# Mixture of experts in a two-layer kernel: 23 chunks of tokens sorted by expert instead of all tokens through all eight experts

## The chip, the cores and the metric

The kernel runs as one launch on one core of a Trainium2 chip. The metric is the device time of one execution in microseconds (us), as the median of repeated runs. Five engines work side by side, each with a queue of its own: TensorE (PE; its weight loads are PEld), VectorE (DVE), ScalarE (ACT), GpSimd (POOL) and SyncE (SP). SyncE, ScalarE and GpSimd also issue DMAs, which 16 DMA engines carry out.

## The reference

`x` has 2 batches of 2048 tokens of 256 features. Layer 0 is causal attention with 16 heads and a mixture of 8 experts, layer 1 a Toeplitz mixing of tokens and a gated feed-forward. Each of the four parts works on a normalised, modulated copy of `x` and is added back through a gate. Changed is the mixture:

```python
logits = einsum('bsd,de->bse', x, gate_w) + gate_b
probs = softmax(logits, axis=1)            # over the tokens of a batch
vals, idx = top_k(probs, 2)                # two experts for each token
h = relu(einsum('bsd,edo->ebso', x, w1) + b1[:, None, None, :])
h = relu(einsum('ebso,eop->ebsp', h, w2) + b2[:, None, None, :])
y = relu(einsum('ebso,eop->ebsp', h, w3) + b3[:, None, None, :])
onehot = one_hot(idx, E)
w_tok = einsum('bske,bsk->bse', onehot, vals)
ind = onehot.max(axis=2)
v = einsum('ebso,bse->eo', y, w_tok)       # one vector of 256 for each expert
out = einsum('bse,eo->bso', ind, v)
```

Three layers of 256x256 run over the tokens of each expert. What leaves an expert is one vector, the weighted sum over all its tokens of both batches; a token gets the sum of its two experts' vectors. A token that an expert was not chosen for has weight zero there.

## The kernel before

The phases follow one another: `phase_setup`, `phase_project`, `phase_attention`, `phase_attn_out`, `phase_route`, `phase_experts`, `phase_mix`, `phase_mix_out`, `phase_ffn`. Each is a block in which every engine has its own list of instructions, ordered by semaphores, and ends with all engines together. `x` stays in SBUF. A tile is 128 tokens, a chunk (CH) 512; the 4096 tokens are 8 chunks.

`phase_attention` is a hand-placed pipeline of 8 units (4 head groups by 2 batches). SyncE loads the heads, TensorE makes scores and running maxima, VectorE reduces maxima out of PSUM, ScalarE takes exponentials and copies finished outputs to `at_oc` (two buffers, L803), and GpSimd stores these to `d_o` (L623). Apart from one memset GpSimd does nothing else there. A unit has four outputs, in the order of 16, 12, 8 and 4 steps of the scores.

`phase_route` goes over the 8 chunks. For each, VectorE normalises (`ln_rows`, with a square root on ScalarE between its parts), TensorE transposes (L1116), ScalarE modulates to `ro_hf` (L1089), TensorE multiplies with the gate (L1126), ScalarE moves the logits to `ro_lg` (L1097), and GpSimd splits `ro_hf` into a high and a low f16 half, `hh_all` and `hl_all` (L1041, L1044), which stay in SBUF. VectorE has only the normalising in this loop. After it come the maxima over each batch, exponentials, scaling, transposes of the probabilities (L1135), the rank of each expert by all pairs of experts (L1072 to L1078), transposes of the indicator into `chosen`, and the weights `ro_wt`, which go to DRAM (L1028).

`phase_experts` goes over experts two at a time, and over 8 chunks of all 4096 tokens for each: 64 chunks of three layers. f32 is imitated by three f16 products (high by high, low by high, high by low), so a layer of a chunk is 12 matmuls of 128x512 and a chunk 36. `SEQ` sets the order on TensorE: in step s the first layer of chunk s, the second of chunk s-1, the third of chunk s-2. ScalarE adds bias and takes the relu into `ex_hf` (L1284), VectorE splits it (L1309, L1311); after the third layer VectorE multiplies by the token weights `ex_wb` (L1320, two instructions a chunk), which counts `dve_y`, and ScalarE takes the relu and sums (L1294). SyncE loads an expert's weights, biases and weights of all tokens once per expert, and GpSimd splits the weights (L1219, L1222). At the end two transposes and 32 tiles of small matmuls put the sums back on `x`.

## Time and profile before

| | |
|---|---|
| three runs | 2364.79, 2368.13 and 2371.26 us, median 2368.13 |
| profiled execution | 2367.53 us, of which the span is 2365.8 us |
| mean granted TensorE clock | 0.924 |
| busy in the span | PE 1989.2 (84%), PEld 957.3, DVE 1444.7 (61%), ACT 960.8 (41%), POOL 171.1 (7%) |
| DMA | 133.46 MB, mean 56 GB/s |

The span is the part of the execution that the profile records. Busy time is the time in which an engine runs at least one instruction. The granted clock is a share of full speed, 2.4 GHz; 0.5 is 1.2 GHz. Each group of instructions is named by line, engine, operation and output<-inputs. "Idle before" is the idle time of that engine just ahead of the group, and what ended it.

### The profile page before, as it was taken

How to read it: one execution, taken by the hardware profiler on the slowest of the kernel's cores; microseconds unless marked ns; L12 is line 12 of the kernel's file. 1: busy time of each engine (PE TensorE's matmuls, PEld its weight loads, DVE VectorE, ACT ScalarE, POOL GpSimd, SP SyncE). 2: the span in 40 equal slices, each digit the busy share in tenths (PEclk: the TensorE clock that was granted, in tenths of full speed). 3: DMA queues.
4: the chain of work that ended last, by engine and by line, in shares of the span. 5: the costliest groups of instructions: out<-in, count | busy, mean ns of one | idle time of the engine just before them, and what ended most of it. 6: DMA issues, size and time to landing. Idle time of an engine off the chain costs nothing. (4 is left out here: it accounts for less than half of the span.)

```text
span 2365.8 us, 37426 instructions
## 1 busy us (share of the span) xinstructions
PE 1989.2 (84%) x13666; PEld 957.3 (40%) x13666; DVE 1444.7 (61%) x3303; ACT 960.8 (41%) x1432; POOL 171.1 (7%) x133
## 2 busy tenths in 40 slices
PE   3773488999989999999956539999999998799978
PEld 3331022333333332333324214444444455699656
DVE  4664788787868787878302446767666655300366
ACT  0331045666666665666740224444444432100133
POOL 1001000000000000000003421111111000000011
PEclk8897599999999999999987669999999988899989
DMA  5236400303030303030013020111111000475001
GB/s 179 74 142 141 80 1 10 55 11 55 11 56 10 59 11 55 11 55 11 10 34 132 0 88 13 50 49 49 49 49 49 0 0 5 148 233 191 1 30 51
DMA packets 69129, 133.46 MB, mean 56 GB/s; under 512 B 9017, under 2 KB 52058, under 8 KB 62682
## 3 DMA queue, kind: packets, MB, share of 16 engines
q1 hardware_dynamic: 65344, 120.85, 18.5%
q0 software_dynamic: 2560, 8.39, 1.0%
q10 hardware_dynamic: 1090, 2.36, 0.3%
q8 instruction: 92, 1.51, 0.3%
q14 instruction: 43, 0.35, 0.1%
HBM read 99.83 MB, written 30.56 MB: 55 GB/s over the span
## 5 line engine op out<-in xcount | busy, mean ns | idle before, releaser
L812 ACT ACTIVATE at_pr<-ps 128x1024 f32<-128x1024 f32 (+3 forms) x640 | 548.8, 894 | 359.7 <-PE ps L752 230.5
L846 DVE TENSOR_REDUCE at_mx<-ps 128x1 f32<-128x512 f32 x768 | 488.8, 685 | 168.1 <-PE ps L702 158.4
L749 PE MATMUL ps<-at_sq,at_sk 64*128 64x512 f16 (+3 forms) x2560 | 344.5, 348 | 20.6 <-DMA at_sq<-at_mr 16.8
L702 PE MATMUL ps<-at_sk,at_sq 64*128 64x512 f16 (+3 forms) x1280 | 236.1, 365 | 112.3 <-DMA at_vl<-d_va 41.0
L728 PE MATMUL ps<-at_pr,at_vl 128*32 128x512 f32 (+3 forms) x2560 | 301.8, 543 | 0.5 <-issue 0.4
L1284 ACT ACTIVATE ex_hf<-ps,ex_bias 128x512 f32<-128x512 f32 x256 | 162.1, 684 | 282.0 <-PE ps L1253 243.8
L843 DVE CUSTOM_DVE_ANT_0 at_seen<-ps,later 128x384 bf16<-128x384 f32 (+3 forms) x512 | 229.9, 487 | 7.0 <-issue 5.3
L702 PEld LDWEIGHTS ps<-at_sk,at_sq 64*128 64x128 f16 x1280 | 62.0, 93 | 409.6 <-DVE at_mx L846 219.1
L752 PE MATMUL ps<-bq,bk 64*128 64x512 f16 (+3 forms) x1280 | 224.5, 347 | 0.0
L1253 PE MATMUL ps<-ex_hh,ex_wh 128*128 128x512 f16 x512 | 194.7, 380 | 12.5 <-DVE ex_hl L1311 11.6
L1309 DVE CAST ex_hh<-ex_hf 128x1024 f16<-128x1024 f32 x128 | 96.0, 750 | 165.7 <-ACT ex_hf L1284 165.7
L1253 PE MATMUL ps<-ex_hh,ex_wl 128*128 128x512 f16 x512 | 194.6, 380 | 0.0
L1253 PE MATMUL ps<-ex_hl,ex_wh 128*128 128x512 f16 x512 | 194.6, 380 | 0.0
L1311 DVE TENSOR_TENSOR ex_hl<-ex_hf,ex_hh 128x1024 f16<-128x1024 f32 x128 | 170.6, 1333 | 4.4
L749 PEld LDWEIGHTS ps<-at_sq,at_sk 64*128 64x128 f16 x2560 | 112.2, 95 | 126.3 <-ACT at_pr L812 35.7
L1516 PE MATMUL ps<-mi_vn,mi_tz 128*128 x1024 | 144.0, 303 | 1.3 <-DMA mi_tz<-d_z 1.3
L1516 PEld LDWEIGHTS ps<-mi_vn,mi_tz 128*128 128x128 f32 x1024 | 141.4, 191 | 4.1 <-issue 1.7
L1253 PE MATMUL ps<-hh_all,ex_wh 128*128 128x512 f16 x256 | 97.7, 382 | 20.5 <-POOL ex_wl L1222 15.7
L1253 PE MATMUL ps<-hh_all,ex_wl 128*128 128x512 f16 x256 | 97.8, 382 | 0.0
L1253 PE MATMUL ps<-hl_all,ex_wh 128*128 128x512 f16 x256 | 97.7, 382 | 0.0
L1441 DVE COPY mixed<-ps 128x256 f32 x32 | 13.6, 424 | 131.5 <-PE ps L1516 131.5
L1320 DVE SCALAR_TENSOR_TENSOR ex_h<-ps,ex_bias,ex_wb 128x512 f32<-128x512 f32 x128 | 89.8, 743 | 6.2 <-PE ps L1253 6.2
(199 smaller groups left out, 2114.8 us busy)
## 6 DMA issues: line engine op xcount, KB each, us to landing
mi_tz<-d_z SPq DMA_DIRECT2D x32, 1024.0 KB, 5.1
ex_wb<-d_wt SPq DMA_DIRECT2D x8, 2048.0 KB, 9.5
d_va<-pj_va SPq DMA_DIRECT2D x8, 1024.0 KB, 3.9
at_vl<-d_va SPq DMA_DIRECT2D x8, 1024.0 KB, 12.6
d_o<-at_oc POOLq DMA_DIRECT2D x32, 256.0 KB, 2.3
ex_w<-in_w SPq DMA_DIRECT2D x24, 256.0 KB, 3.1
x<-in_x SPq DMA_DIRECT2D x2, 2048.0 KB
at_sq<-d_qh SPq DMA_DIRECT2D x32, 128.0 KB, 8.3
```

The source lines that it names most:

```text
L702: ins = pe.matmul(ps[:, MAXB + (slot + r) % RING, 0:hi_ - lo], sq[half[r], b, i, 0, qb * P:(qb + 1) * P], sk[half[r], b, i, 0, lo:hi_], st ...
L728: ins = pe.matmul(ps[32 * h:32 * h + 32, O, off:CH], vl[:, b, kb, 32 * h:32 * h + 32], pr[:, n % 2, h // 2, h % 2, off:CH], start=(kb == 0 ...
L749: pe.matmul(ps[:, 2 * f + r, off:CH], sk[half[r], b, f, part, k], sq[half[r], b, f, part, q], start=part == 0, stop=False)
L752: ins = pe.matmul(ps[:, 2 * f + r, off:CH], g.bk[half[r], b, k], g.bq[half[r], b, q], start=False, stop=t < 0)
L812: act.activation(pr[:, n % 2, f, :, off:CH], ps[:, 2 * f:2 * f + 2, off:CH], ACT.Exp, scale=INV_SCALE).then_inc(exp_done[f], 1)
L843: ins = dve.tensor_tensor_reduce(seen[:, turn, r, 0:n], src, g.later[:, CH - n:CH], 1.0, LOWEST, ALU.add, ALU.max, dst)
L846: ins = dve.tensor_reduce(dst, src, AX.X, ALU.max)
L1253: ins = pe.matmul(ps[:, 2 * PAIR[l, cc] + o, :], lhs, rhs, start=(i == 0), stop=(i == len(parts) - 1))
L1284: ins = act.activation(hf[l][:, o, :], ps[:, 2 * PAIR[l, cc] + o, :], ACT.Relu, bias=bias[:, cc // NC_, l, o:o + 1])
L1309: dve.tensor_copy(hh[l][:, cc % 2], hf[l][:, :, :]).then_inc(high[l], 1)
L1311: dve.tensor_tensor(hl[l][:, cc % 2], hf[l][:, :, :], hh[l][:, cc % 2], ALU.subtract)\
L1516: ins = pe.matmul(ps[:, 2 * p + b, d * HD:C], tz[:, p, b, d * P:(d + 1) * P], vn[:, b * NT:(b + 1) * NT - d, bass.ds((it * 2 + p) * HD, HD ...
```

## The change

- **Weights**: in `phase_attention` GpSimd loads each of the 24 expert matrices, splits it into f16 halves and stores them in `d_w`; it also writes zeros over all of `d_rows`, one piece after each store of `at_oc`.
- **Routing**: TensorE transposes the modulated chunk back to token rows; ScalarE copies the high half and VectorE takes the low half, into a row of 264 words per token (`rows`: 512 f16 values, a weight, padding). The rank of all pairs becomes two rounds of a maximum with ties broken by a falling weight. Two matmuls count the tokens ahead of each; a scan over tiles and one over experts make a position for each token and choice, with each expert's range starting on a multiple of 512.
- **Scatter**: GpSimd scatters the 32 tiles of `rows` by the first choice, then by the second, each an indirect DMA of 128 rows to `d_rows`. VectorE puts in the second weight when the first scatter of eight tiles has landed.
- **Experts**: 23 chunks (NCK = 8192/512 + 7) of `d_rows`, each with its owner's weights; four buffers. Every chunk loads its weights (786 KB), its rows transposed (524 KB), and its 512 weights, first packed together in DRAM, then broadcast. All 23 chunks are always worked through. The tail sums the vectors of each expert's chunks with a small matmul.

```diff
+NCK = NB * T * 2 // CH + E - 1
+ROW = C + 8
@@ phase_attention, gpsimd
+            pool.wait_ge(ld[0], 16 * NLD)
+            fetch(0)
+            for n in range(3 * E):
+                e, l = divmod(n, 3)
+                x = n % 2
+                if n + 1 < 3 * E:
+                    fetch(n + 1)
+                pool.wait_ge(pw_ld[x], 16 * (n // 2 + 1))
+                if n >= 2:
+                    pool.wait_ge(pw_st[x], 16 * (n // 2))
+                pool.tensor_tensor(ph[:, x, 0], pw[:, x], one[:, :, :].to_broadcast([P, KT, C]), ALU.mult)\
+                    .then_inc(pw_high, 1)
+                pool.wait_ge(pw_high, n + 1)
+                pool.tensor_tensor(ph[:, x, 1], pw[:, x], ph[:, x, 0], ALU.subtract).then_inc(pw_split[x], 1)
+                pool.wait_ge(pw_split[x], n // 2 + 1)
+                size = 2 * KT * C
+                pool.dma_start(g.d_w[e, :, l * size:(l + 1) * size], ph[:, x].rearrange("p h k c -> p (h k c)"))\
+                    .then_inc(pw_st[x], 16)
...
+                    pool.dma_start(d_fill[:, bass.ds(u * (NCH * NIL) + i * NIL, NIL)], nil[:, :]).then_inc(filled, 16)
@@ phase_route, gpsimd
+            for i in range(2):
+                pool.wait_ge(idx_ready[i], 1)
+                for t in range(TT):
+                    if t % GROUP == 0:
+                        pool.wait_ge(wt_ready, 1 if i == 0 else 2 + t // GROUP)
+                    pool.indirect_dma_start(g.d_rows, bass.IndirectOffsetOnAxis(ap=idx[i][:, t:t + 1], axis=0),
+                                            rows[:, t, :], None).then_inc(moved[t // GROUP] if i == 0 else again, 16)
+            pool.wait_ge(again, 16 * TT)
@@ phase_route, vector
+            def low(n):
+                dve.wait_ge(hi_ready, n + 1)
+                r = half[:, n * TPC:(n + 1) * TPC, :]
+                dve.tensor_tensor(r[:, :, C:2 * C], ps[:, 4:6, :].rearrange("p a (t c) -> p (a t) c", c=C),
+                                  r[:, :, 0:C], ALU.subtract).then_inc(lo_ready, 1)
...
+            normalise(0)
+            for n in range(N):
+                b = n // NCH
+                if n + 1 < N:
+                    normalise(n + 1)
+                low(n)
+                dve.wait_ge(lg_ready, n + 1)
+                ins = dve.tensor_reduce(cmax[:, n:n + 1], lg[:, b, (n % NCH) * CH:(n % NCH + 1) * CH], AX.X, ALU.max)
...
+            for i in range(2):
+                ch.link(dve.tensor_reduce(best[i][:, :], pn[:, :, :], AX.X, ALU.max))
...
+            ch.link(dve.tensor_tensor_scan(cum[:, :, :].rearrange("p e t -> p (e t)"), tot[:, :, :].rearrange("p e t -> p (e t)"),
+                                           zeros[:, :], 0.0, ALU.add, ALU.add))
@@ phase_route, tensor
+            for n in range(N):
+                if n + 1 < N:
+                    transposes(n + 1)
+                pe.wait_ge(ht_ready, 2 * n + 2)
+                if n:
+                    pe.wait_ge(lg_ready, n)
+                for k in range(KT):
+                    ins = pe.matmul(ps[0:E, 6, :], gw[:, k, :], hf[:, n % 2, k, :], start=(k == 0), stop=(k == KT - 1))
+                ins.then_inc(gate_done, 1)
+                if n:
+                    pe.wait_ge(lo_ready, n)
+                for t in range(TPC):
+                    for k in range(KT):
+                        o = (t % 2) * C + k * P
+                        ins = pe.transpose(ps[:, 4 + t // 2, o:o + P], hf[:, n % 2, k, t * P:(t + 1) * P], g.ident[:, :])
+                ins.then_inc(back_done, 1)
@@ phase_experts, sync
+            def pack(cc):
+                if cc >= 2:
+                    sp.wait_ge(wb_ld[(cc - 2) % BUF], 16 * ((cc - 2) // BUF + 1))
+                sp.dma_start(g.d_ws[cc % 2].unsqueeze(1), g.d_rows[cc * CH:(cc + 1) * CH, C:C + 1],
+                             allow_slow_non_contiguous=True).then_inc(packed[cc % 2], 16)
+
+            pack(0)
+            for cc in range(NCK):
+                x = cc % BUF
+                if cc >= BUF:
+                    sp.wait_ge(dve_y, cc - BUF + 1)
+                e = sp.value_load(g.owner[0:1, cc:cc + 1], min_val=0, max_val=E - 1)
+                sp.dma_start(w[:, x].rearrange("p l h k c -> p (l h k c)"),
+                             g.d_w[bass.ds(e, 1)].rearrange("e p n -> p (e n)")).then_inc(w_ld[x], 16)
+                sp.dma_start(bias[:, x], g.i["b"][bass.ds(e, 1)].rearrange("e p l k -> p (e l) k")).then_inc(w_ld[x], 16)
+                sp.dma_start_transpose(xt[:, x], g.d_rows[cc * CH:(cc + 1) * CH, 0:C].bitcast(F16)).then_inc(x_ld[x], 16)
+                if cc + 1 < NCK:
+                    pack(cc + 1)
+                sp.wait_ge(packed[cc % 2], 16 * (cc // 2 + 1))
+                sp.dma_start(wb[:, x], g.d_ws[cc % 2:cc % 2 + 1, :].bitcast(F32).to_broadcast([P, CH]))\
+                  .then_inc(wb_ld[x], 16)
```

## Rows read from the trace of the kernel before

**Rows 1.** Busy time of each engine in four stretches of time.

```profile
core 0: us, PE busy (x) PEld busy (x) DVE busy (x) ACT busy (x) POOL busy (x), PEclk, DMA share, GB/s
240.00:361.00 121.00, 78.51 (x544) 21.24 (x546) 94.34 (x273) 33.56 (x37) 0.22 (x1) 0.74 0.21 32
1296.00:1366.00 70.00, 37.78 (x96) 14.26 (x96) 35.07 (x115) 21.51 (x34) 32.37 (x17) 0.68 0.00 1
1410.00:1932.00 522.00, 502.67 (x2304) 224.89 (x2302) 351.31 (x391) 240.32 (x510) 66.41 (x46) 0.99 0.11 42
1967.00:2046.00 79.00, 61.20 (x224) 36.06 (x224) 40.60 (x120) 22.86 (x36) 0.00 (x0) 0.85 0.09 23
```

**Rows 2.** The page's costliest groups: busy, mean ns | idle before, what ended it.

```profile
L1253 PE MATMUL ps<-hh_all,ex_wh 128*128 128x512 f16 x256 | 97.7, 382 | 20.5 <-POOL ex_wl L1222 15.7
```

**Rows 3.** Order of time, the experts' edges: start us, duration us, engine, line.

```profile
1404.41 1.43 SPq L1203 DMA_DIRECT2D ex_w<-in_w  x3
...
1409.79 0.58 PE L1253 MATMUL ps<-hh_all,ex_wh 128*128 128x512 f16 x1 [15.73 <-POOL ex_wl L1222]
...
1929.54 0.38 PE L1253 MATMUL ps<-ex_hl,ex_wh 128*128 128x512 f16 x1
```

**Rows 4.** Order of time, first turns of the routing loop.

```profile
1296.65 1.41 DVE L69 BATCH_NORM_STATS2 ro_st<-x 128x6 f32 x4 [0.63 <-SPq L1023]
...
1299.06 1.38 DVE L78 TENSOR_SCALAR ro_hn<-x,ro_mv,ro_rs 128x256 f32 x4
...
1300.49 1.97 PE L1116 MATMUL ps<-ident,ro_hn 128*128 128x128 f32 x8 [5.19 <-DVE ro_hn L78]
...
1303.71 4.57 DVE L78 TENSOR_SCALAR ro_hn<-x,ro_mv,ro_rs 128x256 f32 x4
...
1310.30 3.58 PE L1126 MATMUL ps<-ro_hf,ro_gw 128*8 128x512 f32 x4
```

**Rows 5.** Order of time, the tail of the routing.

```profile
1366.45 2.00 ACT L1102 ACTIVATE ro_lg<-ro_lg,ro_nmax 8x2048 f32<-8x2048 f32 x1
...
1370.74 2.47 DVE L1065 TENSOR_SCALAR ro_lg<-ro_lg,ro_grec 8x2048 f32<-8x2048 f32 x2
1372.07 3.48 PEld L1135 LDWEIGHTS ps<-ident,ro_lg 8*128 8x128 f32 x32 [8.64 <-DVE ro_lg L1065]
...
1385.33 2.29 DVE L1077 TENSOR_REDUCE ro_rank<-ro_wins 128x256 f32<-128x2048 f32 x1
1387.65 0.29 DVE L1078 TENSOR_SCALAR ro_pn<-ro_rank 128x256 f32<-128x256 f32 x1
...
1399.24 0.32 SPq L1028 DMA_DIRECT2D d_wt<-ro_wt  x1
```

**Rows 6.** DMA: a dense stretch; a 1 MB load; the queue from 600 to 720 us.

```profile
2050.00:2060.00 10.00, 10.00 (x75) 9.82 (x74) 0.86 (x3) 0.00 (x0) 0.00 (x0) 1.00 0.91 322
...
mi_tz<-d_z SPq DMA_DIRECT2D x32, 1024.0 KB, 5.1
...
q1 hardware_dynamic: 2768, 2.64, 14.1%
```

**Rows 7.** Two VectorE instructions of the experts: duration ns min/median/max.

```profile
L1320 DVE SCALAR_TENSOR_TENSOR ex_h<-ps,ex_bias,ex_wb x128: 734/743/752, 1433.5 to 1930.6; 128x512 f32<-128x512 f32 x128
...
L1311 DVE TENSOR_TENSOR ex_hl<-ex_hf,ex_hh x128: 1224/1226/2062, 1418.9 to 1925.9; 128x1024 f16<-128x1024 f32 x128
```

**Rows 8.** GpSimd's stores and splits, ScalarE's `at_oc`, and the stores' landing.

```profile
L623 POOL DMA_DIRECT2D d_o<-at_oc x32: 539/539/710, 360.8 to 1216.3; - x32
...
DMA to landing us min/median/max: 2.3/2.3/6.6
...
L803 ACT ACTIVATE at_oc<-ps x32: 591/603/605, 359.9 to 1215.4; 128x512 f32<-128x512 f32 x32
...
L1222 POOL TENSOR_TENSOR ex_wl<-ex_w,ex_wh 128x512 f16<-128x512 f32 x24 | 35.4, 1477 | 1.9
```

**Rows 9.** Widths of work like that added: duration ns min/median/max.

```profile
L812 ACT ACTIVATE at_pr<-ps x640: 377/1024/1055, 290.8 to 1214.4; 128x1024 f32<-128x1024 f32 x128, 128x512 f32<-128x512 f32 x32
...
L355 DVE TENSOR_TENSOR pj_lo<-ps,pj_hi x32: 680/691/692, 68.0 to 202.8; 128x512 f16<-128x512 f32 x32
```

More of the change, by code:

```diff
@@ L12 @@
 BF16 = mybir.dt.bfloat16
+I32 = mybir.dt.int32
 P = 128
@@ L1011, in phase_route @@
[L1011 to L1017 removed]
+        pn = sb("pn", [P, TT, E])
@@ new lines, in _ @@
+            ch.link(dve.tensor_reduce(which[:, :], below[:, :, :], AX.X, ALU.add))
+            dve.tensor_scalar(g.owner[:, :], which[:, :], float(E - 1), None, ALU.min)
+            ch.link(dve.tensor_scalar(g.owns[:, :], cumch[0:NCK, :], lane[0:NCK, 0:1], None, ALU.is_gt))
+            ch.link(dve.scalar_tensor_tensor(g.owns[:, :], first[0:NCK, :], lane[0:NCK, 0:1], g.owns[:, :], ALU.is_le,
+                                             ALU.mult))
+            for j in range(TT // GROUP):
+                dve.wait_ge(moved[j], 16 * GROUP)
+                tiles = slice(j * GROUP, (j + 1) * GROUP)
+                dve.tensor_copy(weight[:, tiles, :], best[1][:, tiles].unsqueeze(2))\
+                   .then_inc(wt_ready, 1)
```

515 lines of the change are left out of this document (273 added, 242 removed).

## The prediction

> **What bounds the kernel now.** I first cut the span into stages by the program's lines and read each stage's engines [rows 1]. The stage of the experts (1410 to 1932 us) is the one that the change shrinks: TensorE is busy 502.67 of 522 us at a granted clock of 0.99, so nearly full speed, while VectorE has 351 us and ScalarE 240 us. The groups by line say the same from the other side: the idle time in front of the matmuls is small, and what ended it is a weight split on GpSimd at the start [rows 2]. So this stage is worth its matmuls: 64 chunks (8 experts by 8 chunks of 512 tokens) of 36 matmuls. 502.67 us by 2304 is 0.218 us each, 7.85 us a chunk. The stage runs from the first weight load at 1404.41 to the last matmul at 1929.54, with the first matmul at 1409.79 [rows 3]: 5.4 us of feed, then 520 us.
>
> The stage of routing is of another kind. From 1296 to 1366 no engine is busy for more than 54% of it and TensorE's clock is 0.68 [rows 1]: it is a chain of hand-offs. The order of time shows a turn of its loop: LayerNorm on VectorE, eight transposes on TensorE 3.8 us after its start, the gate's matmuls later [rows 4]. Then a tail to 1399.24, where the expert weights are stored, and the next stage's first load 5.2 us behind it [rows 3, 5].
>
> **The experts, with the matmuls alone.** 23 chunks of the same 36 matmuls: 23 x 7.85 = 181 us. VectorE's work for a chunk is 351/64 = 5.5 us [rows 1], the same instructions as before, and stays under TensorE's. Fill and drain of the pipeline I put at 10 us (the before kernel has them four times within its 520).
>
> **The feed of a chunk.** Before, weights were loaded once in 8 chunks, and tokens lay in SBUF. Now SyncE issues six things a chunk: reading the owner, 786 KB of weights, a small bias, a transposing load of 524 KB, 512 single words copied within DRAM (`pack`), and 262 KB of broadcast weights. Of these only plain loads have rows. With the 16 DMA engines 91% busy they moved 322 GB/s, so 354 GB/s full; 1 MB lands 5.1 us after issue, thus some 2 us fixed and 3 us of moving [rows 6]. Weights and broadcast cost 3.0 us of moving a chunk. The transposing load I bound from below by plain speed, 1.5 us. From above: it takes 2048 runs of 256 bytes; the short rows of an attention stretch took 14.1% of 16 x 120 us for 2768 packets, 98 ns each [rows 6]; 2048 x 98 ns over 16 engines is 12.5 us. The pack by the same price is at most 3.1 us, at least nothing worth counting. I take 4 us for the transpose, nearer the lower end: the rows that give 98 ns are of loads that write 16 partitions at a time (`at_sq`, `at_sk`), and this one writes all 128 like the plain ones, and 1 us for the pack: 3.0 + 4 + 1 = 8 us of DMA a chunk, about TensorE's own 7.85.
>
> The Trainium skill, *DMA: Bandwidth & Descriptors*, section on latency and other measured facts, gives 261 GB/s for a DMA transpose with a non-contiguous middle dimension; by it this one moves in 2.0 us, and the sum below would be some 23 us lower. No row here shows a transposing DMA.
>
> What decides is not that rate but the lead. There are four buffers, and buffer `x` is free when `dve_y` of chunk cc-4 has been counted. In `SEQ`, layer 3 of chunk cc-4 is the last slot of step cc-2, and layer 1 of chunk cc the first of step cc. Between them lie one step of TensorE (7.85 us) less the two VectorE instructions that free the buffer (0.743 each, 1.5 us, [rows 7]): 6.35 us of lead. The feed needs L = 1 (semaphore and value load, not shown; bounds 0.2 and 2.3, the latter being a whole DMA's landing, [rows 8]) + 0.4 issue + 2.0 fixed + 2.2 for the weights + 4 for the transpose = 9.6 us. Two stalls share the gap, one in front of each step, so the period is 7.85 + (9.6 - 6.35)/2 = 9.5 us. TensorE is then 83% busy. The stage at 77% busy (1967 to 2046) had a clock of 0.85 and the experts at 96% had 0.99 [rows 1], so I add a little, for a period of 9.7 us. The stage: 9.6 for the first feed + 23 x 9.7 + 10 = 243 us, against 525.1. **Gain 282 us.** Bounds: period 7.85 with a feed of 7 us gives 198 us (gain 327); a period of 18.6 us of DMA (3.0 + 12.5 + 3.1) gives 448 (gain 77).
>
> **The routing loop.** The GpSimd splits go; VectorE's `ro_hn` instructions, which took 4.57 us beside them, return to the 1.38 us that four take alone [rows 4]. But the loop closes tighter. In the new VectorE order, `normalise(n+1)` comes, then `low(n)`, which waits for ScalarE's high half, which waits for the back transposes, which stand in TensorE's queue behind `transposes(n+1)` and the gate. Nothing of turn n+1 begins before turn n's `low`. One turn: LayerNorm 3.8 (1296.65 to 1300.49); eight transposes 2.0; two gate matmuls 1.8 (3.58 for four); eight back transposes 2.0 [rows 4]; ScalarE's copy of 128x1024 out of PSUM 1.0; `low` of the same size, twice 0.69, 1.4 [rows 9]; the maximum over 512 columns 0.6 (2.29 for 2048, [rows 5]); five hand-offs 0.8. That is 13.4 us. Seven such turns, 3.8 us in front and 8 us for the last give 106; the softmax of batch 0 inside it adds 4 (exponential 2.0, scaling 1.2, its share of table loads). 110 us from 1296.65 ends at 1406.7. Before, the last logits were there at about 1365. **Loss 41 us.** Hardly less than 95, hardly more than 125.
>
> **Positions.** Softmax of batch 1: exponential 2.2, scaling 1.3, 16 transposes 1.8, a copy and hand-offs: 6.4 us [rows 5]. Then eleven picking instructions on 128x256, each 0.3 to 0.4 (0.29 for one; 2.29 for eight times the elements, [rows 5]), 4.7 us; two counting matmuls and their hand-off 1.2; copy, scan, sums and some fourteen small ones 4.9. The first scatter starts near 1406.7 + 17 = 1424. The transposes into `chosen`, owners and second weights run under the scatters.
>
> **The scatters.** 64 indirect DMAs of 128 rows, one after the other on GpSimd, and the stage cannot end before them. Not shown by the trace. Below: a plain 128-row DMA holds GpSimd 0.539 us. Above: each would wait for its landing, 0.54 + 2.3 = 2.8 us [rows 8]. I take 1.2: the issue is software's, now with an index to read per row, but no wait stands between them. 77 us, to 1501; with 5.2 us of stage end the experts begin at 1506 instead of 1404.4. **Loss 102 us** for the whole routing stage (bounds 60 and 204).
>
> **Attention.** GpSimd gets 24 weight splits ahead of its stores of `at_oc`. Each: two issues 1.1, two elementwise instructions of 1.48 [rows 8], 0.3 of waits, 4.4 us; from 240 they end at 345. The first store is due at 360 [rows 8], and ScalarE waits only before the third (two `oc` buffers), twenty steps of the scores later: no loss. Does GpSimd slow VectorE there? VectorE reads PSUM in this stretch; in the experts `ex_h<-ps`, with GpSimd busy beside it part of the time, took 734 to 752 ns throughout, while `ex_hl<-ex_hf`, from SBUF to SBUF, went from 1224 to 2062 [rows 7]. I count nothing; if VectorE were held for the whole 105 us by half, it would be 50. Weight traffic and the zero fills (12 MB in 32 pieces) meet 21% and less of DMA use [rows 1]. The last fill ends the stage 1.5 us later. One barrier more and the sum over chunks cost 3 us.
>
> **Sum.** The profiled execution took 2367.5 us around its span of 2365.8, and the median of the three runs is 2368.1, so no correction: 2367.5 - 282 + 102 + 1.5 + 3 = 2192 us. A difference under 0.3% (7 us) counts as no change.
>
> **Rivals.**
> - *Feed hidden, scatters cheap (0.15).* Period 7.85 and 0.54 us a scatter: 2192 - 45 - 42 = 2105. For it: plain loads ran at 354 GB/s. Against: only 6.35 us of lead.
> - *The feed as the bound (0.15).* Period 14 us, short runs half way to their worst: 2192 + 4.3 x 23 = 2291. TensorE would sit near 55% busy, waiting for `ex_xt`.
> - *Scatters wait (0.10).* 2.8 us each: 2192 + 102 = 2294. Against: before's stores carry no such wait.
> - *The clock falls (0.07).* With a gap in each chunk TensorE is granted 0.5, as between 240 and 361 it had 0.74 at 65% busy [rows 1]; 36 matmuls take 15.7 us, period 15.7: 2192 + 138 = 2330.
> - *Slower (0.08).* Short runs at full price, in the transposing load and the pack: period 18.6, 2192 + 205 = 2397. It decides from a period of 17.4 us on ((2367.5 - 2192)/23 + 9.7).
> - *The gain doesn't come (0.02)*: within 7 us, by several of these together.
> - *Forecast (0.43)*, 2150 to 2250.
>
> On the slower rival, the same page of the Trainium skill says in its rules for kernel authors that a strided last dimension becomes one descriptor per element, and should be made contiguous. That rule speaks against `pack`, and no row here shows a DMA of single words.
>
> **Numbers.** Range 2110 to 2330: the feed and scatter rivals are inside, the slower one and half of the cheap one outside. Faster 0.89, same 0.02, slower 0.09.
>
> **What would show it.** The experts' stage near 243 us, TensorE some 80% busy, waiting in front of each chunk for `ex_xt` or `ex_w`. The routing loop with a turn of 13 us, TensorE's clock low. 64 GpSimd DMAs 1.2 us apart while VectorE is idle. The first `d_o` store still at 360. Wrong it would be most easily through the two prices no row gives: a transposing load of over 8 us, or a scatter of over 2 us.

## The result, and the profile after

The changed kernel takes 2255.7 us (median of 4 runs, 2248.09 to 2256.95), the kernel before 2367.9 us in the same comparison. The ratio is 0.9519 with a 95% interval of 0.9502 to 0.9536, so 112 us are gained where 176 were forecast. The time lies inside the stated range of 2110 to 2330 us, but 6 us above the case held most likely (2150 to 2250). One term, the period of a chunk in the experts, came out a quarter longer than forecast, and for a reason that the forecast did not have.

The first lines of the page, and the groups of its costliest instructions that belong to the change:

```profile
span 2252.9 us, 33869 instructions
...
PE 1705.8 (76%) x12260; PEld 828.4 (37%) x12260; DVE 1213.8 (54%) x3100; ACT 817.1 (36%) x1114; POOL 234.8 (10%) x264
...
L1383 PE MATMUL ps<-ex_xt,ex_w 128*128 128x512 f16 x276 | 86.7, 480 | 182.8 <-DMA ex_xt<-d_rows 117.2
...
L1112 POOL DMA_INDIRECT d_rows<-ro_rows,ro_idx x64 | 62.0, 969 | 140.4 <-DVE ro_idx L1192 121.2
```

TensorE is idle for 182.8 us ahead of the matmuls that read `ex_xt`. Before, the group of [rows 2] had 20.5 us. About 104 of the 182.8 are the one wait for the first chunk, behind the scatters. The rest, some 78 us, falls on 22 chunks.

The busy time of each engine in four stretches: attention beside GpSimd's weight splits, the routing loop, the scatters, and the experts. They answer to [rows 1].

```profile
core 0: us, PE busy (x) PEld busy (x) DVE busy (x) ACT busy (x) POOL busy (x), PEclk, DMA share, GB/s
242.00:361.00 119.00, 75.40 (x532) 20.54 (x532) 92.99 (x267) 32.71 (x35) 84.45 (x96) 0.74 0.53 139
1303.00:1405.00 102.00, 49.45 (x176) 24.05 (x176) 42.23 (x132) 35.68 (x47) 0.70 (x3) 0.68 0.01 1
1425.00:1507.00 82.00, 0.00 (x0) 0.00 (x0) 1.93 (x10) 0.00 (x0) 62.01 (x64) 0.51 0.29 105
1527.00:1813.00 286.00, 206.50 (x828) 85.01 (x828) 117.57 (x137) 85.09 (x180) 0.00 (x0) 0.90 0.76 123
```

In the experts' stretch TensorE is busy for 72% (206.50 of 286 us), at a granted clock of 0.90. VectorE and ScalarE are far from full, and so is the DMA in bytes (123 GB/s). Yet the DMA engines are busy for 76% of the time: they hold packets that take long, as shown below. The first row shows that attention did not suffer: VectorE 92.99 of 119 us with GpSimd busy for 84 of them, against 94.34 of 121 before.

The queue of SyncE in the experts' stage, in order of time (start, duration, line), for one chunk and the start of the next:

```profile
1599.87 0.33 SPq L1355 DMA_DIRECT2D ex_w<-d_w  x1
1600.39 0.34 SPq L1357 DMA_DIRECT2D ex_bias<-in_b  x1
1600.77 8.39 SPq L1358 DMA_TRANSPOSE ex_xt<-d_rows  x1
1609.21 0.59 SPq L1346 DMA_DIRECT2D d_ws<-d_rows  x1
1609.84 0.61 SPq L1362 DMA_DIRECT2D ex_wb<-d_ws  x1
1612.28 0.33 SPq L1355 DMA_DIRECT2D ex_w<-d_w  x1
```

And the DMA issues of the stage (KB each, median us from issue to landing), with the transposing load by itself:

```profile
ex_w<-d_w SPq DMA_DIRECT2D x21, 768.0 KB, 9.7
ex_wb<-d_ws SPq DMA_DIRECT2D x21, 256.0 KB, 8.0
...
ex_xt<-d_rows SPq DMA_TRANSPOSE x21, 10.9
d_ws<-d_rows SPq DMA_DIRECT2D x20, 2.0 KB, 8.5
```

```profile
L1358 SPq DMA_TRANSPOSE ex_xt<-d_rows x23: 3476/8639/10067, 1516.6 to 1781.5; - x23
...
DMA to landing us min/median/max: 5.5/10.9/14.5
```

Landing is the moment at which all data of a DMA has arrived. The transposing load holds SyncE for 8.6 us (median), but once for only 3.48 us. The weights, 786 KB, land 9.7 us after their issue, where the 1 MB of [rows 6] took 5.1. Of the turn of 12.4 us between these two weight loads SyncE spends 10.3 issuing. So the bound is not the wait for a free buffer, on which my working rested: in the stretch 1560 to 1780 that wait (for `ex_h`) stands in the queue 9 times, for 8.9 us in all.

**Stage by stage.** Times are starts read from the order of time.

| stage | forecast | measured |
|---|---|---|
| arrival at the routing stage | +1.5 us | +6.7 us (1303.05 for 1296.31) |
| routing loop to the last maximum | 110 us | 101.5 us |
| positions, to the first scatter | 17.3 us | 20.3 us |
| 64 scatters | 77 us | 81.2 us |
| end of the stage, to the first DMA of the next | 5.2 us | 7.2 us |
| experts, first load to last matmul | 243 us | 299 us |
| after it, and the barrier | +3 us | +4 us |

A turn of the routing loop, in order of time:

```profile
1321.04 1.38 DVE L72 BATCH_NORM_STATS2 ro_st<-x 128x6 f32<-128x256 f32 x4
...
1324.86 1.97 PE L1253 MATMUL ps<-ident,ro_hn 128*128 128x128 f32 x8 [6.65 <-DVE ro_hn L81]
...
1326.76 3.58 PE L1273 MATMUL ps<-ro_hf,ro_gw 128*8 128x512 f32 x4
...
1330.27 1.45 PE L1280 MATMUL ps<-ident,ro_hf 128*128 128x128 f32 x8
...
1331.76 1.02 ACT L1235 ACTIVATE ro_rows<-ps 128x1024 f16<-128x1024 f32 x1 [0.71 <-PE ps L1280]
...
1332.81 1.23 DVE L1130 TENSOR_TENSOR ro_rows<-ps,ro_rows 128x1024 f16<-128x1024 f32 x1 [8.01 <-ACT ro_rows L1235]
1333.95 0.66 DVE L1145 TENSOR_REDUCE ro_cmax<-ro_lg 8x1 f32<-8x512 f32 x1
1334.55 1.39 DVE L72 BATCH_NORM_STATS2 ro_st<-x 128x6 f32<-128x256 f32 x4
```

The chain is the forecast one, link by link, and its length (13.5 us) is the forecast 13.4. VectorE stands for 8.01 us in front of `low` (L1130). The 8 us by which the whole loop was shorter than forecast have two sources. The seven turns took 94.2 us where 97.8 were forecast with the softmax of batch 0: two of them took 11.9, the first of these at a granted clock of 0.72 where the turn shown had 0.63. And the last chunk, behind which nothing more is normalised, came 3.5 us after the one before it, where 8 were forecast.

### The profile page after: what moved, and what is told of

Same layout as the page of the kernel before. It is cut to its first block and busy times, and to the rows that moved or that the text cites. A ratio compares the mean times of both kernels' runs of the same rounds, so it can differ in the third digit from the quotient of the medians.

```text
span 2252.9 us, 33869 instructions
## 1 busy us (share of the span) xinstructions
PE 1705.8 (76%) x12260; PEld 828.4 (37%) x12260; DVE 1213.8 (54%) x3100; ACT 817.1 (36%) x1114; POOL 234.8 (10%) x264
## 5 line engine op out<-in xcount | busy, mean ns | idle before, releaser
L858 ACT ACTIVATE at_pr<-ps 128x1024 f32<-128x1024 f32 (+3 forms) x640 | 548.6, 894 | 359.9 <-PE ps L798 231.4
L1383 PE MATMUL ps<-ex_xt,ex_w 128*128 128x512 f16 x276 | 86.7, 480 | 182.8 <-DMA ex_xt<-d_rows 117.2
L1414 ACT ACTIVATE ex_hf<-ps,ex_bias 128x512 f32<-128x512 f32 x92 | 58.2, 683 | 301.9 <-PE ps L1383 301.9
L1434 DVE CAST ex_hh<-ex_hf 128x1024 f16<-128x1024 f32 x46 | 31.9, 694 | 225.2 <-ACT ex_hf L1414 225.2
L1383 PEld LDWEIGHTS ps<-ex_xt,ex_w 128*128 128x128 f16 x276 | 30.6, 116 | 236.4 <-issue 220.9
L1383 PE MATMUL ps<-ex_hh,ex_w 128*128 128x512 f16 x368 | 110.2, 381 | 0.8 <-DVE ex_hl L1436 0.8
L665 POOL DMA_DIRECT2D d_o<-at_oc x32 | 17.3, 541 | 830.0 <-ACT at_oc L849 807.2
L1561 DVE COPY mixed<-ps 128x256 f32 x32 | 13.6, 425 | 134.0 <-PE ps L1636 134.0
L798 PEld LDWEIGHTS ps<-bq,bk 64*128 64x128 f16 x1280 | 62.8, 95 | 59.4 <-issue 2.6
L1693 ACT ACTIVATE mo_at<-ps 128x512 f32<-128x512 f32 x16 | 8.7, 594 | 200.4 <-PE ps L1664 200.4
L774 PEld LDWEIGHTS ps<-at_pr,at_vl 128*32 128x32 f32 x2560 | 50.8, 108 | 78.8 <-issue 63.1
L1112 POOL DMA_INDIRECT d_rows<-ro_rows,ro_idx x64 | 62.0, 969 | 140.4 <-DVE ro_idx L1192 121.2
```

The lines of the kernel that those rows point to most:

```text
L774: ins = pe.matmul(ps[32 * h:32 * h + 32, O, off:CH], vl[:, b, kb, 32 * h:32 * h + 32], pr[:, n % 2, h // 2, h % 2, off:CH], start=(kb == 0 ...
L798: ins = pe.matmul(ps[:, 2 * f + r, off:CH], g.bk[half[r], b, k], g.bq[half[r], b, q], start=False, stop=t < 0)
L858: act.activation(pr[:, n % 2, f, :, off:CH], ps[:, 2 * f:2 * f + 2, off:CH], ACT.Exp, scale=INV_SCALE).then_inc(exp_done[f], 1)
L1112: pool.indirect_dma_start(g.d_rows, bass.IndirectOffsetOnAxis(ap=idx[i][:, t:t + 1], axis=0), rows[:, t, :], None).then_inc(moved[t // GRO ...
L1383: ins = pe.matmul(ps[:, 2 * PAIR[l, cc] + o, :], lhs, rhs, start=(i == 0), stop=(i == len(parts) - 1))
L1414: ins = act.activation(hf[l][:, o, :], ps[:, 2 * PAIR[l, cc] + o, :], ACT.Relu, bias=bias[:, cc % BUF, l, o:o + 1])
```

## The experiments

Each kernel's time is from one run and its profile; only the changed kernel (four runs) and *g1* (five) have more. The kernel before, timed beside them, took 2364 to 2370 us. The changed kernel's own runs lie 9 us apart, so a few us between two rows are no effect. *e1*, *e2*, *f1* and *g4* load other data or leave transfers out, so they compute other numbers and serve for their time alone. The **period** is worked out the same way everywhere: the start of the last matmul on `ex_xt`, less 2.4 us for the eleven before it in its chunk, less the start of the first, by 22. For the changed kernel that is (1798.3 - 2.4 - 1527.1)/22 = 12.2 us. The landings in the table are medians over the whole stage; those in the DMA lines below are over 1540 to 1800 us and can differ a little.

| kernel | us | period | `ex_w` lands | `ex_xt` lands | TensorE busy, 1560 to 1740 |
|---|---|---|---|---|---|
| changed kernel | 2255.7 | 12.2 | 9.7 | 10.9 | 132 of 180 |
| e1, plain rows | 2227.1 | 10.9 | 7.4 | 9.6 | 142 |
| e2, no weights | 2228.2 | 11.0 | - | 9.5 | 141 |
| e3, rows first | 2260.2 | 12.1 | 5.4 | 10.5 | 128 |
| e4, weights by GpSimd | 2272.7 | 13.0 | 12.1 | 12.4 | 124 |
| f1, no pack | 2184.6 | 9.2 | 4.8 | 6.2 | 160 |
| f2, pack twice | 2283.4 | 13.6 | 10.6 | 12.0 | 122 |
| f3, pack once | 2169.7 | 8.7 | 4.6 | 5.8 | 160 |
| f4, routing ahead | 2225.7 | 12.9 | 10.1 | 11.5 | 127 |
| g2, pack through SBUF | 2169.9 | 8.8 | 4.7 | 5.9 | 157 |
| g3, pack by GpSimd | 2248.8 | 12.0 | 5.8 | 11.3 | 131 |
| g4, pack of two rows | 2168.6 | 8.6 | 4.6 | 5.7 | 160 |

**First theories.** The profile after offered three readings of the long period. T1: it is the issue of the transposing load that holds SyncE. T2: weights and rows collide on their way. T3: the throughput of the DMA engines is spent. The first four kernels were made to tell these apart.

*e1*, the rows loaded plainly, in the same size:

```diff
-                sp.dma_start_transpose(xt[:, x], g.d_rows[cc * CH:(cc + 1) * CH, 0:C].bitcast(F16)).then_inc(x_ld[x], 16)
+                sp.dma_start(xt[:, x], g.d_rows[cc * CH:(cc + 1) * CH, 0:C].bitcast(F16).rearrange("(a p) c -> p a c", p=P)).then_inc(x_ld[x], 16)
```

> The rows of a chunk are loaded with a plain DMA of the same bytes, not transposed (so the experts work on other numbers; the instructions are the same). Three theories for the period of 12.2 us a chunk, where 9.7 was forecast. T1, issue: DMA_TRANSPOSE holds SyncE for 8.6 us whatever else goes on, and the period is the sum of what SyncE issues. T2, collision: the weights of a chunk and its transposing load, issued right behind them, get in each other's way, and both are cheap alone. T3, throughput: the 16 DMA engines are full (share 0.81 with the gaps between). All three expect the period to fall to TensorE's 7.9 to 8.3 us here, so 2165 us; it tells what the transposing load costs in all. If it stays near 12, the transpose isn't the cause and all three fall.

Measured 2227.1 us. That is a gain of 29 us. All three theories had it near 2165, so each of them promised three times that. The plain load holds SyncE for 0.43 us only, and yet the rows land in 9.6 us.

*e2*, the weights loaded for the first four chunks only:

```diff
-                sp.dma_start(w[:, x].rearrange("p l h k c -> p (l h k c)"),
-                             g.d_w[bass.ds(e, 1)].rearrange("e p n -> p (e n)")).then_inc(w_ld[x], 16)
+                if cc < BUF:
+                    sp.dma_start(w[:, x].rearrange("p l h k c -> p (l h k c)"),
+                                 g.d_w[bass.ds(e, 1)].rearrange("e p n -> p (e n)")).then_inc(w_ld[x], 16)
...
-                    pe.wait_ge(w_ld[x], 32 * (cc // BUF + 1))
+                    pe.wait_ge(w_ld[x], 16 * (cc // BUF + 2))
```

> Weights are loaded for the first four chunks only and used again for the rest (which leaves out 19 of 23 weight loads). T1 expects the period to fall only by the issue of one DMA, 0.5 us, to 11.7: 2245 us, with DMA_TRANSPOSE still near 8.6 us. T2 expects DMA_TRANSPOSE to shorten to about the 3.5 us that its shortest instance took, and the period to come to TensorE's, 7.9 to 8.5: 2165 to 2175 us. T3 expects the period to fall by the weights' share of the DMA engines, to about 7 of transfer, also TensorE's pace, but with DMA_TRANSPOSE still waiting for full queues in the first chunks.

Measured 2228.2 us. The largest transfer of the chunk is gone, the engines move 78 GB/s in the place of 130, and the period is still 11.0 us. Neither the throughput in bytes nor a collision of the two large loads can be the main cause: no weights are left for the rows to collide with, and they still land in 9.5 us.

*e3*, the rows issued ahead of the value load, the weights and the biases:

```diff
+                sp.dma_start_transpose(xt[:, x], g.d_rows[cc * CH:(cc + 1) * CH, 0:C].bitcast(F16)).then_inc(x_ld[x], 16)
                 e = sp.value_load(g.owner[0:1, cc:cc + 1], min_val=0, max_val=E - 1)
...
-                sp.dma_start_transpose(xt[:, x], g.d_rows[cc * CH:(cc + 1) * CH, 0:C].bitcast(F16)).then_inc(x_ld[x], 16)
```

> Only the order changes: the transposing load of a chunk is issued first, then the owner is read and the weights and bias loaded. Same bytes, same instructions. T1 and T3 expect no change: period 12.2 us, 2250 to 2260 us. T2 expects less, since the weights no longer stand right in front of the transposing load: a period of 8.5 to 10.5, 2170 to 2215 us, and DMA_TRANSPOSE near 3.5 us.

Measured 2260.2 us, the same time, but another picture in the DMA issues:

```profile
ex_w<-d_w SPq DMA_DIRECT2D x21, 768.0 KB, 4.7
...
ex_xt<-d_rows SPq DMA_TRANSPOSE x21, 10.4
```

The weights, now second, land in 4.7 us in the place of 9.7 (5.4 over the whole stage), and their place behind the pack has gone to the rows. SyncE is held by the transposing load for only 4.6 us (median), and the period stays. So the delay belongs to the *position* behind the pack and the broadcast, not to a transfer and not to the hold. This row made the fourth theory.

*e4*, the value load, the weights and the biases moved to GpSimd's queue:

```diff
+        @block.gpsimd
+        def _(pool):
+            for cc in range(NCK):
+                x = cc % BUF
+                if cc >= BUF:
+                    pool.wait_ge(dve_y, cc - BUF + 1)
+                e = pool.value_load(g.owner[0:1, cc:cc + 1], min_val=0, max_val=E - 1)
+                pool.dma_start(w[:, x].rearrange("p l h k c -> p (l h k c)"),
...
```

> Weights and bias of a chunk are issued by GpSimd, which is idle in the experts; SyncE keeps the transposing load, the packing and the broadcast. T1 expects SyncE's sum without 0.35 + 0.35 + 1.4 us of value load: period 10 us, 2205 us. T2 expects it to depend on whether the two still meet in the DMA engines; where they do, DMA_TRANSPOSE stays near 8 us. T3 expects no change in the DMA engines' time, so a period of 10 to 12 us and the share of the DMA engines near 1.

Measured 2272.7 us, 17 us worse. The weights now land in 12.1 us, the transposing load held SyncE for up to 21.2 us, and a second queue bought nothing. Taking work off SyncE is no cure either, so none of the three readings survives these four kernels as the main cause.

**The fourth theory (T4):** `pack`, the copy of 512 single words from DRAM to DRAM in each chunk, holds up whatever comes next on the DMA engines. The prediction had given it 1 us of moving. Its rivals are T5, that the weights' own reads are slow, and T6, that the broadcast of the token weights holds things up.

*f1*, the pack only for the first two chunks:

```diff
-                if cc >= 2:
-                    sp.wait_ge(wb_ld[(cc - 2) % BUF], 16 * ((cc - 2) // BUF + 1))
-                sp.dma_start(g.d_ws[cc % 2].unsqueeze(1), g.d_rows[cc * CH:(cc + 1) * CH, C:C + 1],
-                             allow_slow_non_contiguous=True).then_inc(packed[cc % 2], 16)
+                if cc < 2:
+                    sp.dma_start(g.d_ws[cc % 2].unsqueeze(1), g.d_rows[cc * CH:(cc + 1) * CH, C:C + 1],
+                                 allow_slow_non_contiguous=True).then_inc(packed[cc % 2], 16)
...
-                sp.wait_ge(packed[cc % 2], 16 * (cc // 2 + 1))
+                sp.wait_ge(packed[cc % 2], 16)
```

> Only the first two chunks' weights are packed; the other 21 chunks broadcast those again (so the copy of 512 single words within DRAM is left out 21 times, and the token weights are the wrong ones). With the transpose out, with the weights out and with the order turned, the period stayed at 10.9, 11.0 and 12.1 us: none of issue, throughput or the meeting of weights and rows explains it alone. T4: the 512 single-word writes of the packing come out of the engines' queues fast but hold up what follows on them; the weights of the next chunk, 3 us of transfer, take 8 to 10 us to land because their first packets stand still for 4 to 6. T4 expects the weights to land in 4 to 5 us (now 9.7), DMA_TRANSPOSE in 3.5 to 5 us, and a period of 8 to 9: 2165 to 2190 us. T5, the weights' own reads are slow whatever goes before: they still land in 9 to 10 us, period above 11.5. T6, the broadcast (128 reads of the same 2 KB) holds things up: as T5, since it stays.

Measured 2184.6 us: 71 us from 21 copies of 2 KB. The landing of the weights, and the transposing load by itself:

```profile
ex_w<-d_w SPq DMA_DIRECT2D x20, 768.0 KB, 4.8
...
L1357 SPq DMA_TRANSPOSE ex_xt<-d_rows x23: 3228/3858/8676, 1513.8 to 1718.7; - x23
```

Everything else in the stage became fast with it. The weights land in 4.8 us and the transposing load takes 3.9 us of SyncE in the place of 8.6. T5 and T6, which expected a period above 11.5, fall: it is 9.2.

The single packets of the two traces show what changed. In the changed kernel's stage, 403 of 2816 packets of the weights (6144 bytes each) took more than 1.5 us, the longest 7.1; in *g4* below, where the pack takes another form, it was 1. Half of all took at most 0.23 us in both. Around 1612 us one sees it happen: the pack's words pass from 1610.5 to 1612.9, each in 9 ns, which is 0.3 us for 512 of them on 16 engines, and the first 16 packets of the weights, from 1613.2 on, take 2.5 to 5.4 us. In *f3* below, between 1610.5 and 1610.9, the first 16 of a chunk took 0.3 to 1.3 us. In *e3*, where the rows stand behind the pack, the rows' packets of 256 bytes are hit: 50 ns on average for 22 in f3, and of the weights' packets only 1 took more than 1.5 us. So the words themselves are cheap, and what stands behind them is not. By the share of busy DMA engines (0.81 between 1560 and 1740) a chunk costs them 0.81 x 12.2 = 9.9 us. In f3 (0.74 between 1520 and 1714) it is 0.74 x 8.7 = 6.4 us. The difference, 3.5 us, is the difference of the periods.

*f2*, the pack issued a second time, into a buffer of its own:

```diff
                 sp.dma_start(g.d_ws[cc % 2].unsqueeze(1), g.d_rows[cc * CH:(cc + 1) * CH, C:C + 1],
                              allow_slow_non_contiguous=True).then_inc(packed[cc % 2], 16)
+                sp.dma_start(g.d_wx[cc % 2].unsqueeze(1), g.d_rows[cc * CH:(cc + 1) * CH, C:C + 1],
+                             allow_slow_non_contiguous=True).then_inc(packed[cc % 2], 16)
...
-                sp.wait_ge(packed[cc % 2], 16 * (cc // 2 + 1))
+                sp.wait_ge(packed[cc % 2], 32 * (cc // 2 + 1))
...
```

> The packing of each chunk is done twice, the second time into another place. T4 expects some 4 to 6 us more a chunk, so a period of 16 to 18 us: 2345 to 2390 us. T5 and T6, and a packing that costs only its issue and its packets (0.6 us and 0.3 us), expect a period near 13: 2265 to 2275 us.

Measured 2283.4 us and a period of 13.6, so 1.4 us more a chunk, where T4 had said 4 to 6 and its rivals about 1. The first pack costs 3 to 3.5 us of period and the second 1.4. The price does not go by the number of words, and why not is open.

*f3* leaves nothing out. The words of all chunks are packed once, by ScalarE's queue at the start of the stage, into SBUF and from there to DRAM as runs of 368 bytes. Each chunk then only broadcasts its row, one turn later:

```diff
...
+            def broadcast(cc):
+                if cc == 0:
+                    sp.wait_ge(packed[1], 16)
+                sp.dma_start(wb[:, cc % BUF], g.d_ws[cc:cc + 1, :].bitcast(F32).to_broadcast([P, CH]))\
+                  .then_inc(wb_ld[cc % BUF], 16)
...
-                if cc + 1 < NCK:
-                    pack(cc + 1)
-                sp.wait_ge(packed[cc % 2], 16 * (cc // 2 + 1))
-                sp.dma_start(wb[:, x], g.d_ws[cc % 2:cc % 2 + 1, :].bitcast(F32).to_broadcast([P, CH]))\
-                  .then_inc(wb_ld[x], 16)
+                if cc:
+                    broadcast(cc - 1)
+            broadcast(NCK - 1)
...
+            act.dma_start(wsb[:, :].unsqueeze(2), g.d_rows[:, C:C + 1].rearrange("(p n) o -> p n o", p=P),
+                          allow_slow_non_contiguous=True).then_inc(packed[0], 16)
+            act.wait_ge(packed[0], 16)
+            act.dma_start(g.d_ws.rearrange("k n -> (k n)").rearrange("(p n) -> p n", p=P), wsb[:, :])\
+               .then_inc(packed[1], 16)
...
```

> A whole kernel: all 23 chunks' weights are packed once at the start of the experts, DRAM to SBUF (11776 single words read, written to 128 partitions) and from there to DRAM in rows of 368 bytes, both issued by ScalarE; each chunk then only broadcasts its row. T4 expects the same as without packing, period 8 to 9, plus up to 10 us at the start where the words meet the first loads: 2170 to 2200 us. T5 and T6 expect a period above 11.5, 2245 us or more.

Measured 2169.7 us, 86 us under the changed kernel. Its queue of SyncE, for one chunk and the start of the next:

```profile
1600.27 0.34 SPq L1355 DMA_DIRECT2D ex_w<-d_w  x1
...
1601.16 3.34 SPq L1358 DMA_TRANSPOSE ex_xt<-d_rows  x1
1604.55 0.57 SPq L1347 DMA_DIRECT2D ex_wb<-d_ws  x1
1609.55 0.34 SPq L1355 DMA_DIRECT2D ex_w<-d_w  x1
```

Here is the wait that the prediction had put at the centre. From 1605.1 SyncE waits for a free buffer. VectorE's `ex_h` ends at 1608.8, the weights are issued at 1609.55, the rows at 1610.46, and TensorE starts on them at 1616.02. So the feed L of the prediction is 7.2 us, and by the prediction's formula the period is 7.85 + (7.2 - 6.35)/2 = 8.3 us; measured 8.7.

**Which part of the pack costs?** Three kernels change the pack, each in another way.

*g2*: as many single words are read each chunk, but into SBUF (128 partitions by four), and go to DRAM a turn later as 128 runs of 16 bytes. The wait for `packed` moves ahead of the two:

```diff
+            def words(cc):
+                sp.dma_start(wsb[:, cc % 2, :].unsqueeze(2),
+                             g.d_rows[cc * CH:(cc + 1) * CH, C:C + 1].rearrange("(p n) o -> p n o", p=P),
+                             allow_slow_non_contiguous=True).then_inc(loaded[cc % 2], 16)
...
-                sp.dma_start(g.d_ws[cc % 2].unsqueeze(1), g.d_rows[cc * CH:(cc + 1) * CH, C:C + 1],
-                             allow_slow_non_contiguous=True).then_inc(packed[cc % 2], 16)
+                sp.dma_start(g.d_ws[cc % 2].rearrange("(p n) -> p n", p=P), wsb[:, cc % 2, :])\
+                  .then_inc(packed[cc % 2], 16)
...
+                sp.wait_ge(packed[cc % 2], 16 * (cc // 2 + 1))
+                if cc + 2 < NCK:
+                    words(cc + 2)
                 if cc + 1 < NCK:
                     pack(cc + 1)
-                sp.wait_ge(packed[cc % 2], 16 * (cc // 2 + 1))
...
```

> The copy of 512 single words a chunk stays, but goes through SBUF: the words into 128 partitions of four, a turn later 128 runs of four words back to DRAM, then the broadcast as before. As many single words are read, none is written singly to DRAM. If single-word writes to DRAM hold up the queues, the period falls from 12.2 to about 9 to 9.5 us and the time to 2180 to 2195. If the number of single words in the queues does it, whichever way they go, the period stays at 12 or more: 2255 to 2290.

*g3*: the same copy, issued by GpSimd, whose queue is empty in this stage:

```diff
-                if cc + 1 < NCK:
-                    pack(cc + 1)
...
+        @block.gpsimd
+        def _(pool):
+            for cc in range(NCK):
+                if cc >= 2:
+                    pool.wait_ge(wb_ld[(cc - 2) % BUF], 16 * ((cc - 2) // BUF + 1))
+                pool.dma_start(g.d_ws[cc % 2].unsqueeze(1), g.d_rows[cc * CH:(cc + 1) * CH, C:C + 1],
+                               allow_slow_non_contiguous=True).then_inc(packed[cc % 2], 16)
```

> The same copy of single words from DRAM to DRAM, at the same place in the sequence, but issued by GpSimd into its own queue, where nothing else stands in this stage. If what it holds up is what stands behind it in SyncE's queue, the weights land in 4.6 to 5 us again and the time falls to 2175 to 2195. If the words hold up the engines or the memory for every queue, the weights still land in 9 us or more and the time stays at 2245 to 2270.

*g4*: a copy of the same 2 KB from DRAM to DRAM in the same place, as two runs of 1 KB:

```diff
-                sp.dma_start(g.d_ws[cc % 2].unsqueeze(1), g.d_rows[cc * CH:(cc + 1) * CH, C:C + 1],
-                             allow_slow_non_contiguous=True).then_inc(packed[cc % 2], 16)
+                sp.dma_start(g.d_ws[cc % 2].rearrange("(a n) -> a n", a=2),
+                             g.d_rows[cc * CH:cc * CH + 2, 0:C]).then_inc(packed[cc % 2], 16)
```

> The copy of each chunk stays in its place and in its size (2 KB from DRAM to DRAM), but takes two whole runs of 1 KB (the first two rows of the chunk) in place of 512 single words: the shares are left out, the experts' outputs are weighted with other data. If any copy from DRAM to DRAM in front of the weights holds them up, or the wait and the broadcast behind it, the time stays at 2240 to 2260. If the single words do it, 2170 to 2190 and a period of about 8.7 to 9.2 us, as without the copy.

Measured: g2 2169.9 us, g3 2248.8, g4 2168.6. The DMA issues of g2 first, then those of g3, with the DMA time of its two queues (packets, MB, share of the 16 engines; q0 holds GpSimd's), then one line of g4:

```profile
ex_w<-d_w SPq DMA_DIRECT2D x19, 768.0 KB, 4.7
...
d_ws<-ex_wsb SPq DMA_DIRECT2D x19, 2.0 KB, 2.1
...
ex_wsb<-d_rows SPq DMA_DIRECT2D x18, 2.0 KB, 2.5
```

```profile
q1 hardware_dynamic: 52685, 32.69, 74.0%
q0 software_dynamic: 640, 0.04, 0.8%
...
ex_w<-d_w SPq DMA_DIRECT2D x20, 768.0 KB, 5.7
...
ex_xt<-d_rows SPq DMA_TRANSPOSE x21, 11.3
d_ws<-d_rows POOLq DMA_DIRECT2D x20, 2.0 KB, 9.9
```

```profile
ex_w<-d_w SPq DMA_DIRECT2D x19, 768.0 KB, 4.6
```

Reading 512 single words into SBUF takes 2.5 us to landing and disturbs nothing (g2). A copy from DRAM to DRAM in the same place, with the wait and the broadcast behind it, disturbs nothing either when it takes whole runs (g4). What is left is the copy of single words whose source and destination are both DRAM. With it the pack lands in 8.5 us and its neighbours are held up. Whether the single writes alone do it is argued, not shown: no kernel here writes single words from SBUF to DRAM, and g3's pack stands in the trace as 32 packets a chunk, 16 of them of 128 bytes, so that its words are not seen one by one.

A queue of its own does not help. In g3 the copies take 0.8% of the DMA engines' time, the weights are nearly quick (5.7 us), but the rows land in 11.3 us and the period is 12.0; the time, 2248.8 us, lies within the changed kernel's own runs. For such a time I had expected the weights at 9 us or more. They escaped, and the rows were hit.

**The routing loop.** *f4* tests the other large term. `low(n)` and the maximum of chunk n come after `normalise` of chunk n+2 is issued, and ScalarE's square roots go ahead of its waits for the transposes:

```diff
...
+            def finish(n):
+                b = n // NCH
+                low(n)
+                dve.wait_ge(lg_ready, n + 1)
...
                 if n + 1 < N:
                     normalise(n + 1)
-                low(n)
-                dve.wait_ge(lg_ready, n + 1)
...
+                if n:
+                    finish(n - 1)
...
+                if n + 2 < N:
+                    root(n + 2)
                 act.wait_ge(back_done, n + 1)
...
```

> The routing loop's order alone: VectorE takes the low half of chunk n-1 only after it has normalised chunk n+1, and ScalarE takes the square root for chunk n+2 before the high half of chunk n. Same instructions. If the turn of 13.4 us is the chain that the prediction named, it opens, and a turn costs VectorE's 5.7 us plus hand-offs or TensorE's 5.5, 6 to 8 us: the loop falls from 101.5 to 55 to 70 us, 2210 to 2225 us in all. If the turn is bound by something else (TensorE's low clock, one engine's work), it stays near 100 us and the time near 2256.

Measured 2225.7 us, 30 us gained, at the top of what was expected. A turn of its loop, seen on VectorE:

```profile
1330.90 1.38 DVE L72 BATCH_NORM_STATS2 ro_st<-x 128x6 f32<-128x256 f32 x4
...
1334.66 1.22 DVE L1130 TENSOR_TENSOR ro_rows<-ps,ro_rows 128x1024 f16<-128x1024 f32 x1
1335.80 0.66 DVE L1142 TENSOR_REDUCE ro_cmax<-ro_lg 8x1 f32<-8x512 f32 x1
...
1336.57 1.38 DVE L72 BATCH_NORM_STATS2 ro_st<-x 128x6 f32<-128x256 f32 x4
```

The turn is 5.7 us instead of 13.5, and the 8 us wait in front of `low` is gone. The first scatter starts at 1381.4 instead of 1425.0, 43.6 us earlier. But the experts then ran with a period of 12.9 instead of 12.2, and 15 of these us were given back there. The granted clock between 1560 and 1740 was 0.87 there and 0.91 in the changed kernel, and the rows landed in 11.5 us for 10.9. One profile each does not say which came first; it is left open.

*g1* has f3 and f4 together, timed against the kernel before in five rounds.

> The two edits that gained, together: the tokens' shares are packed once behind the routing stage (gained 86 us alone) and the routing loop issues the means of the next chunk ahead of the wait for this chunk's transposes (gained 30 us alone). They lie in different stages. Adding up: 2255.7 - 86 - 30 = 2140 us. Rival: the routing loop's gain is a gain of clock as well as of order, and the experts behind it start at a lower granted clock when the loop is shorter: then 2145 to 2160.

Measured 2129.3 us (2127.2 to 2133.2), a ratio of 0.8986 with an interval of 0.8970 to 0.9002. That is 126 us under the changed kernel, and 11 us less than the 2140 that adding the two gains up had given. Against f3 the first matmul of the experts comes 37.9 us earlier and the last on `ex_xt` 37.2 us: without the pack nothing is handed back, which fits that the gains do more than add up. The rival, which expected 2145 or more for a lower clock, did not come. The granted clock is 0.87 in g1 from 1480 to 1520 and 0.88 in f3 from 1520 to 1560, the first 40 us of the stage in each, and 1.00 behind it in both.

## Why the prediction was right, and where it was off

**The experts: the period.** This is the term that failed, and with it the mechanism of the largest stage. The period was put at 9.7 us and measured 12.2; the stage took 299 us instead of 243. Two errors of opposite sign lie in it. The transposing load and the weights together were put too high: without the pack L was 7.2 us where I had 9.6, and the rows land 5.7 to 5.9 us after issue. The formula with the lead of 6.35 us then gave 8.3 for a measured 8.7, so the step from feed and lead to period held where the pack was gone. The step that broke is "1 us for the pack": it bounded only what the pack itself moves (0 to 3.1 us) and left it out of L. Its moving is small, 0.3 us. What it costs is the time of the transfers next to it: 12.2 - 8.7 = 3.5 us a chunk, most of the 86 us by which f3 is faster.

The pack also changed the kind of bound. In f3 SyncE waits for a buffer, as forecast. In the changed kernel SyncE hangs in the issue of the transposing load (8.6 us for 3.6). That the time still fell inside the range was helped by luck: the range was wide for rivals with other causes, and the 2.4 us too much in L, by the formula 1.2 us of period, covered part of what the pack cost. The sign named beforehand, a transposing load of over 8 us, did come (8.6 us of issue, 10.9 to landing), but its cause is the pack and not the load.

**A rule of the Trainium skill.** The forecast held a rule of the Trainium skill against `pack` (*DMA: Bandwidth & Descriptors*, rules for kernel authors: a strided last dimension becomes one descriptor per element). The direction was right. But g2 keeps 512 single words on the reading side at no cost that shows, 2169.9 us against f3's 2169.7, so here the strided read alone is harmless. The specifications of the same page of the Trainium skill say that a transfer below 512 bytes makes the DMA engine read, modify and write; g2's runs of 16 bytes to DRAM are below it too, and landed in 2.1 us. And the section on issuing engines, on this page of the Trainium skill, says that these are not separate DMA queues, since all of them use the same 16 engines; g3 and e4 agree, with 2248.8 and 2272.7 us for 2255.7. The 261 GB/s that the page of the Trainium skill gives for a transposing load, by which an estimate of 2.0 us follows here, was not tried alone; with its weights beside it, the load landed in 5.8 us.

**The slower rival** had the right place (short runs in the transposing load and the pack) and the wrong price: a period of 18.6 for a measured 12.2. The 256-byte runs of the transposing load were never dear: in f3's trace half of them took at most 18 ns, where the rival had 98. *The feed as the bound* (period 14, 2291 us) is nearer to what happened than the forecast's own mechanism, but its reason, short runs half way to their worst, is not what the runs showed. *The clock falls*: it stood at 0.90 in the stage, not at 0.5. It was not without effect: TensorE's own work was 206.50/23 = 9.0 us a chunk for 7.85 at 0.99. As TensorE waits for its rows as well, what this adds to the period is not separated here.

**The routing loop.** Forecast 110 us, measured 101.5. The turn was right (13.4 and 13.5) by offsetting errors: the gate takes 3.5 us, since the four records of [rows 4] are one turn's and not two, and the back transposes, `low` and the hand-offs take less. What the loop as a whole took less is told above, with its turns. f4 shows that the order was the cause, as said: with `low` moved out of the way of the next turn it is 5.7 us.

**Positions** took 20.3 us for 17.3: VectorE's instructions on 128x256 take 0.42 us each, not 0.3 to 0.4, and the scan 0.69. **Scatters**: 0.97 us each and 0.30 between them, 1.27 for the assumed 1.2. They do not wait for landings. **Attention**: the splits took 1.05 to 1.16 us each for the assumed 1.48, but the first began only at 256.4, when its weights had landed, and not at 240. GpSimd was done near 354, and the first `at_oc` came at 361.3 for 359.9, so the cover held. The routing stage began 6.7 us later than before, for the 1.5 assumed. 2.6 of these are there at attention's first matmul (242.7 for 240.1). GpSimd's first weight load is issued behind it, at 243.3, so that traffic is not the cause, which stays open. 2.9 are there at the last `at_oc`, and nearly 4 more come in between it and the routing stage; the last zero fill ends there, but no run takes it out.

**The sum of the misses**: 56 for the experts, -8.5 for the loop, +3 for positions, +4 for the scatters, +2 for the stage's end, +5 for the arrival, +1 behind it make 63 us, which is what lies between 2192 and the profiled execution (2254.6).

## What to carry to other kernels

Look at what a small DMA does to the others, and not only at what it moves: a landing that doubles on a large transfer, or an issue that stretches on a queue, can have its cause in a 2 KB copy in front of it. Move the suspected transfer by one place in the queue; if the delay passes to another transfer, it belongs to the neighbour. Single words gathered within DRAM are better taken through SBUF, or packed once for all chunks; here either gave 86 us. And where a loop's turn is a chain of hand-offs from engine to engine, issue the next turn's start ahead of this turn's last step; in the routing loop this cut the turn from 13.5 to 5.7 us.

## What was not expected of the hardware

- A copy of 512 four-byte words from DRAM to DRAM costs the transfers around it 3.5 us a chunk, yet twice as many cost only 1.4 us more. Its own packets take 9 ns each; packets of 6144 bytes behind them, 0.23 us in the median, take up to 7.1 us. The same words written to SBUF cost nothing that shows. Why (the single writes, source and destination both in DRAM, or 512 writes into the same 2 KB) is not settled by these runs.
- Issuing the transposing load of 512x512 two-byte elements holds SyncE for about 3.6 us even without the pack (f3: 2.9 to 5.3 us), while the plain load of e1 took 0.43 us.
- An indirect DMA of 128 rows of 1056 bytes holds GpSimd for 0.97 us, and the next starts 0.30 us later; 64 of them ran with no wait for a landing.
- GpSimd's elementwise work beside VectorE's instructions that read PSUM cost nothing that shows: 92.99 of 119 us busy with it, 94.34 of 121 without.
